# A GRU on one core: the reset gate's two halves in one pass in every step of the middle

## The chip, the cores and the metric

The kernel runs on one core of a Trainium2 chip. The metric is the device time of one execution in microseconds (us), lower is better. Each kernel is timed in several runs, and the median counts. TensorE multiplies matrices into the banks of PSUM, ScalarE applies functions, VectorE does the elementwise work, SyncE starts the transfers. Each engine has its own list of instructions and takes them in the order of that list; semaphores tie the lists together.

## The reference

A gated recurrent unit over 128 steps, batch 64, 512 inputs, 512 hidden values. After every fourth step (but not the last) the state goes through one more layer, the propagation. The output is the states plus the input.

```
def step(h, inp):
    x_t, prop = inp
    comb = jnp.concatenate([x_t, h], axis=-1)
    z = jax.nn.sigmoid(comb @ Wz + bz)
    r = jax.nn.sigmoid(comb @ Wr + br)
    comb2 = jnp.concatenate([x_t, r * h], axis=-1)
    h_cand = jnp.tanh(comb2 @ Wh + bh)
    h_new = (1.0 - z) * h + z * h_cand
    h_next = jnp.where(prop, jnp.tanh(h_new @ Wp + bp), h_new)
    return (h_next, h_new)
...
x = x + transpose(ys)
```

## The kernel before

Everything lies transposed: 512 hidden values are four groups of 128 partitions, the 64 batches are columns. Each float32 matrix is split into a high and a low float16 part, and a product is three: low weights by high values, high weights by high values, high weights by low values.

The steps come in 16 blocks of 8 (BLOCK). In the middle of the kernel the products of x with the input weights, for a whole block, are made by seven products instead of eight (a Strassen scheme), for each of three gates: 21 "stages" of 12 matmuls with 256 columns. They are handed out over the eight steps of the block before (STAGES_AT) and fill TensorE while the recurrence waits for ScalarE and VectorE. A step with t % 4 = 3 does the propagation at its end, and has stages both ahead of it and behind it. ScalarE reads most finished stages out of their banks (`read_stage`, L551), VectorE the products 5 and 6 (`end_quarter`, L963), which add to what ScalarE wrote; a later stage that adds to the same bank waits for that (`wait_stage`: product 7 waits for `c22_out`, which the L963 of product 6 tells). Of the stages, numbers 15 to 17 stand in steps with t % 8 = 6 (17 is a product 5), 18 and 19 ahead of the propagation of a step with t % 8 = 7 (19 is a product 6), and 20 (a product 7) behind it.

One step goes so. TensorE: reset product (R), update product (Z), candidate product (C), stages. `seed` (ScalarE, L613 or L622) puts x's share and the bias into a gate's bank before the product adds to it. The middle of a step is a chain across engines: R is squashed, VectorE multiplies by h and splits the result into high and low (`q_split`, L1048, then L1050 and L1026), and only then can C begin.

A gate can be done in two ways:
- apart: the products by the high and by the low values of h are separate matmuls of 64 columns into one half of a bank, and ScalarE squashes the bank itself (`squash`, L591);
- joint, in steps 19 to 108 (JOINT): `rec_both` (L1362) multiplies the high weights by both parts at once, 128 columns, into both halves of the bank. Then the halves must be added: VectorE does a TENSOR_REDUCE (L1043 in two parts for R, L1061 for Z, L1078 for C), and ScalarE squashes the sum from SBUF (`squash_sums`, L585). The seed fills both halves, with half the value (L613, 512 elements a partition, against L622 with 256).

In these steps Z is always joint, C in t % 8 of 1, 4 and 6, and R where this line says:

```
JOINT_RESET_AT = (0, 1, 2, 4, 5, 6)
```

Where R is joint, TensorE also draws the first 4 matmuls of the step's first stage (AHEAD_OF_C) ahead of C.

The order of work is written out by hand: each engine's list is the loop over steps in its own function, and there is no scheduler. Around the change ScalarE's loop has: squash R, split parts of x (`split_slot`, L539, at the steps in SLOT_AT), squash Z, squash C, `seed(R, t + 1)`, `seed(Z, t + 1)`, then, in a step with a propagation, read the stages ahead of it, squash PROP (tanh), read the stage behind it, and `seed(C, t + 1)`. VectorE's loop has: reduce R if joint, q_split and the rest of q, reduce Z, `split_slot` (L890), reduce C if joint, keep (L1082), new (L1102), the state's high part (L1111, named h_split, or q_split ahead of a propagation), h_ring (L1114), its low part (L1026), then add_states (L1031), a sum of x parts (L950), `end_quarter` (L963), and at a propagation h_split from the tanh (L1141).

Of the kernel before, what the change touches and what calls it, by code (L numbers as in the profile page):

```python
# [16 lines left out]
BLOCK = 8  # L17
RING = 4
R, Z, C, PROP = range(4)
# [13 lines left out]
AHEAD = 32  # L33
REC_SUM_AT = 4
EARLY_PROP_SHARE = 1.4
JOINT_RESET_AT = (0, 1, 2, 4, 5, 6)
AHEAD_OF_C = 4
JOINT = range(19, 109)
JOINT_CANDIDATE_AT = (1, 4, 6)
# [16 lines left out]

STAGES_AT = [((), (0, 1)), ((), (2, 3, 4)), ((), (5, 6)), ((7, 8), (9,)), ((), (10, 11, 12)), ((), (13, 14)), ((), (15, 16, 17)), ((18, 19), (20,))]

SLOT_AT = {2: (5, 6, 6, 8, 8, 9, 10), 3: (4, 5, 6, 7, 7, 8, 9)}
SLOT_AT_LATER = (1, 2, 3, 4, 5, 6, 7)  # L60
SUM_AT = {2: (4, 5, 7, 9), 3: (3, 5, 6, 6)}
SUM_AT_LATER = (0, 1, 5, 3)
# [7 lines left out]
def gru_kernel(nc, x, h0, wz, wr, wh, wp, biases, out):  # L70
# [61 lines left out]
    def fill_of(t):  # L132

        first = issued(t - 1) if t else PER_BLOCK + AHEAD
        return first, (first + issued(t) + 1) // 2, issued(t)

    def stages_of(t):

        m, s = divmod(t, BLOCK)
        return STAGES_AT[s] if m + 1 in SEVEN else ((), ())  # L140
# [9 lines left out]
    def slots_at(t):  # L150

        return [(m, slot) for m in SEVEN for slot, s in enumerate(SLOT_AT.get(m, SLOT_AT_LATER)) if BLOCK * (m - 2) + s == t]

# [17 lines left out]
    def wsum_of(t):  # L171

        return divmod(WSUM_AT.index(t), 4) if t in WSUM_AT else (None, None)
# [6 lines left out]
    with ExitStack() as ctx:  # L180
# [186 lines left out]
        def propagates(t):  # L367
            return t % CHUNK == CHUNK - 1 and t < T - 1

        def joint(t):  # L370

            return t in JOINT

        def joint_reset(t):

            return joint(t) and t % BLOCK in JOINT_RESET_AT

# [4 lines left out]
        def resets_before(t):  # L382
            return sum(joint_reset(step) for step in range(t))
# [10 lines left out]
        def props_before(t):  # L394
            return t // CHUNK
# [103 lines left out]
        def _(act):  # L499
# [42 lines left out]
            def split_wsum(g, n):  # L542

                act.wait_ge(wsum_made, 4 * g + n + 1)
                slot, made = WSUMS[n]
                nc.scalar.activation(win_hi[g][:, slot], made[:], ACT.Copy, scale=scale[:, WIN + g:WIN + g + 1]).then_inc(wsum_hi_ready, 1)
# [34 lines left out]
            def squash_sums(g, func, summed, count, halves):  # L581

                for n, half in enumerate(halves):
                    act.wait_ge(summed, count + n + 1)
                    nc.scalar.activation(gate[g][:, half], gate[g][:, half], func, scale=unscale[:, g:g + 1]).then_inc(gate_ready[g], 1)  # L585

            def squash(g, func, count, halves):

                act.wait_ge(product_done[g], count + 1)
                for half in halves:  # L590
                    nc.scalar.activation(gate[g][:, half, :], acc[g][:, half, :], func, scale=unscale[:, g:g + 1]).then_inc(gate_ready[g], 1)  # L591
# [110 lines left out]
            for t in range(T):  # L702
                m, s = divmod(t, BLOCK)
                first, middle, last = (n // PER_GROUP for n in fill_of(t))
                stages_first, stages_last = stages_of(t)
                wsum_gate, wsum_place = wsum_of(t)


                ahead = t == T - 2
                if joint_reset(t):  # L710
                    squash_sums(R, ACT.Sigmoid, reset_summed, 2 * resets_before(t), HALVES)
                else:
                    squash(R, ACT.Sigmoid, t, HALVES)
                if ahead:
                    seed(R, t + 1)

                if t and t % CHUNK == 0 and props_before(t) < T // CHUNK - 1:
                    seed_prop(props_before(t))
                if wsum_gate is not None:
                    split_wsum(wsum_gate, wsum_place)  # L720
                for block_m, slot in slots_at(t):
                    split_slot(block_m, slot)
                if squares_at(t):
                    act.wait_ge(h_prop_ready, 2 * props_before(t) + 2)
                if t >= BLOCK:
                    for block_m, k in squares_at(t):
                        x_squares(block_m, k)
                if joint(t):
                    squash_sums(Z, ACT.Sigmoid, update_summed, JOINT.index(t), WHOLE)
                else:  # L730
                    squash(Z, ACT.Sigmoid, t, WHOLE)
                if ahead:
                    seed(Z, t + 1)
                if joint_candidate(t):
                    squash_sums(C, ACT.Tanh, candidate_summed, 2 * candidates_before(t), HALVES)
                elif t < T - 1:
                    squash(C, ACT.Tanh, t, HALVES)
                else:
                    for n, half in enumerate(HALVES):
                        act.wait_ge(product_done[C], T + n)  # L740
                        nc.scalar.activation(gate[C][:, half, :], acc[LAST_BANKS[half.start]][:, half, :], ACT.Tanh,  # L741
                                             scale=unscale[:, C:C + 1]).then_inc(gate_ready[C], 1)
                late = [g for g in (R, Z) if starts(t + 1) and groups_for(g, t + 1) > first]
                if t + 1 < T and not ahead:
                    for g in (R, Z):
                        if g not in late:
                            seed(g, t + 1)
                if t < BLOCK:
                    for block_m, k in squares_at(t):
                        x_squares(block_m, k)  # L750
                if s in SPLIT_AT and m + 2 == LAST:
                    for k in SPLIT_AT[s]:
                        split_x(m + 2, k)
                if t in (1, 2):
                    split_rec(PROP, t - 1)
                if t == 2:
                    seed_prop(0)
                if propagates(t):
                    for n in range(first, middle):
                        copy_group(n)  # L760
                        seed_behind(n, late, t + 1)
                    for n in stages_first:
                        read_stage(m + 1, n)
                    act.wait_ge(squares_ready, KC + squares_before(t))
                    squash(PROP, ACT.Tanh, props_before(t), HALVES)
                    for n in range(middle, last):
                        copy_group(n)
                        seed_behind(n, late, t + 1)
                    for n in stages_last:
                        read_stage(m + 1, n)  # L770
                else:
                    for n in range(first, last):
                        copy_group(n)
                        seed_behind(n, late, t + 1)
                    for n in stages_last:
                        read_stage(m + 1, n)
                if t + 1 < T:
                    seed(C, t + 1)
# [725 lines left out]
```

## Time and profile before

| | |
|---|---|
| median of 3 runs | 1040.14 us (1040.03 to 1040.64) |
| the profiled execution | 1041.51 us |
| its span, first to last instruction | 1039.6 us |
| TensorE matmuls | 1034.6 us busy, 20938 |
| VectorE | 872.3 us busy |
| ScalarE | 774.0 us busy |
| a step 3 or 7 of a block in the middle | 9.49 us |

The profile is of one execution. Busy times of TensorE are modelled and overlap: a matmul with 64 columns is shown as 193 ns, though the next starts much sooner. How long one really holds the engine is read from the distance of starts. In the timeline neighbours of one kind are merged to a row with their count. A bracket at a row's end tells of idle time of that engine ahead of it, and of what ended it. The granted clock of TensorE is full (1.0) for the whole span.

### The profile page before, as it was taken

The page shows a single profiled execution, that of the slowest core. Times are in us where ns is not written, and L with a number is a line of the kernel's source. Part 1 is how long each engine was busy: PE and PEld are TensorE (multiplying, and loading weights), DVE is VectorE, ACT ScalarE, POOL GpSimd, SP SyncE. Part 2 cuts the span into 40 slices and gives each one's busy share as a digit, 9 for nine tenths or more (in the row PEclk, how much of TensorE's full clock was granted, in tenths as well). Part 3 has the DMA queues.
Part 4 walks back from the last instruction along what each step waited for, and adds up shares of the span by engine and source line. Part 5 has one row for each costly group of instructions (what it writes and reads, how often), then busy time and mean ns, then how long its engine had stood idle before and what let it go on. Part 6 is the DMA issues. An engine that isn't in the chain of part 4 may idle for free.

```text
span 1039.6 us, 48435 instructions
## 1 busy us (share of the span) xinstructions
PE 1034.6 (100%) x20938; PEld 955.2 (92%) x20938; DVE 872.3 (84%) x2856; ACT 774.0 (74%) x1789; POOL 0.2 (0%) x4
## 2 busy tenths in 40 slices
PE   9999999999999999999999999999999999999998
PEld 4577899999999999999999999999999999999998
DVE  6978888898988899888889888998888998776666
ACT  6877777787877777777877777877777777665565
POOL 0000000000000000000000000000000000000000
PEclk9999999999999999999999999999999999999999
DMA  9312211001111011110011110111100100000001
GB/s 329 112 43 84 84 54 44 21 25 43 43 43 34 12 43 43 44 43 23 23 44 43 43 42 7 41 44 43 44 24 23 43 23 22 24 8 19 24 24 45
DMA packets 38486, 47.29 MB, mean 45 GB/s; under 512 B 2176, under 2 KB 34048, under 8 KB 37888
## 3 DMA queue, kind: packets, MB, share of 16 engines
q1 hardware_dynamic: 38000, 44.12, 12.6%
q8 instruction: 165, 2.70, 1.1%
q14 instruction: 49, 0.40, 0.1%
q10 hardware_dynamic: 272, 0.07, 0.0%
HBM read 27.40 MB, written 16.78 MB: 42 GB/s over the span
## 4 chain that ended last, share of the span: by engine, by line
PE 100%; DVE 0%; issue 0%; ACT 0%; DVEq 0%
PE acc L1354 39%; PE x_acc L1268 34%; PE acc L1362 16%; PE x_acc L1158 8%; PE x_acc L1289 1%; PE acc L1282 0%; PE x_acc L1276 0%; ACT gate L741 0%; DVE new L1093 0%; PE acc L1164 0%; DVE x_blk L1097 0%; DVEq L180 0%; DVE sum_over L967 0%
## 5 line engine op out<-in xcount | busy, mean ns | idle before, releaser
L1268 PE MATMUL x_acc<-x_hi,win_hi 128*128 128x256 f16 x1092 | 297.7, 273 | 0.0
L1268 PE MATMUL x_acc<-x_lo,win_hi 128*128 128x256 f16 x1092 | 297.6, 273 | 0.0
L1268 PE MATMUL x_acc<-x_hi,win_lo 128*128 128x256 f16 x1092 | 297.6, 273 | 0.0
L585 ACT ACTIVATE gate<-gate,unscale 128x128 f32<-128x128 f32 (+1 forms) x292 | 119.8, 435 | 123.7 <-DVE gate L1061 78.2
L591 ACT ACTIVATE gate<-acc,unscale 128x128 f32<-128x128 f32 (+1 forms) x408 | 131.2, 370 | 99.6 <-PE acc L1354 99.4
L1354 PE MATMUL acc<-h_split,wrec_lo 128*128 128x64 f16 x4096 | 181.2, 193 | 0.1
L551 ACT ACTIVATE x_part<-x_acc,bias,part_unscale 128x256 f32<-128x256 f32 x312 | 154.5, 560 | 19.1 <-PE x_acc L1268 19.1
L1362 PE MATMUL acc<-h_split,wrec_hi 128*128 128x128 f16 x2512 | 166.0, 219 | 0.0
L1354 PE MATMUL acc<-q_split,wrec_hi 128*128 128x64 f16 x4000 | 162.0, 193 | 0.3 <-issue 0.3
L1354 PEld LDWEIGHTS acc<-h_split,wrec_lo 128*128 128x128 f16 x4096 | 155.4, 98 | 5.2 <-issue 0.5
L1362 PEld LDWEIGHTS acc<-h_split,wrec_hi 128*128 128x128 f16 x2512 | 142.8, 98 | 0.0
L1354 PEld LDWEIGHTS acc<-q_split,wrec_hi 128*128 128x128 f16 x4000 | 136.5, 98 | 0.4 <-issue 0.4
L1354 PE MATMUL acc<-h_split,wrec_hi 128*128 128x64 f16 x3168 | 134.5, 193 | 0.0
L613 ACT ACTIVATE acc<-x_part,half_seed_scale 128x512 f32<-128x512 f32 x191 | 126.0, 685 | 0.0
L1354 PE MATMUL acc<-q_split,wrec_lo 128*128 128x64 f16 x2544 | 120.6, 193 | 0.0
L1268 PEld LDWEIGHTS x_acc<-x_hi,win_lo 128*128 128x128 f16 x1092 | 106.8, 98 | 11.3
L1268 PEld LDWEIGHTS x_acc<-x_hi,win_hi 128*128 128x128 f16 x1092 | 106.8, 98 | 10.7
L1268 PEld LDWEIGHTS x_acc<-x_lo,win_hi 128*128 128x128 f16 x1092 | 106.9, 98 | 10.1
L1354 PEld LDWEIGHTS acc<-h_split,wrec_hi 128*128 128x128 f16 x3168 | 110.1, 98 | 0.0
L1354 PEld LDWEIGHTS acc<-q_split,wrec_lo 128*128 128x128 f16 x2544 | 98.6, 98 | 5.0
L1048 DVE TENSOR_TENSOR q_split<-gate,h_ring 128x128 f16<-128x128 f32 x192 | 54.3, 292 | 54.2 <-ACT gate L591 46.5
L622 ACT ACTIVATE acc<-x_part,seed_scale 128x256 f32<-128x256 f32 x192 | 88.7, 477 | 1.8
(141 smaller groups left out, 1509.5 us busy)
## 6 DMA issues: line engine op xcount, KB each, us to landing
out_dram<-x_blk SPq DMA_DIRECT2D x30, 512.0 KB, 3.3
x_blk<-x_dram SPq DMA_DIRECT2D x24, 512.0 KB, 3.8
x_blk<-x_dram SPq DMA_DIRECT2D x3, 1024.0 KB, 8.5
x_part<-wz_dram SPq DMA_DIRECT2D x4, 256.0 KB, 6.5
x_part<-wh_dram SPq DMA_DIRECT2D x4, 256.0 KB, 6.3
x_part<-wr_dram SPq DMA_DIRECT2D x1, 1024.0 KB, 10.7
x_part<-wz_dram SPq DMA_DIRECT2D x1, 1024.0 KB, 12.9
x_part<-wh_dram SPq DMA_DIRECT2D x1, 1024.0 KB, 15.4
```

Source lines behind the costliest of these rows:

```text
L551: nc.scalar.activation(part_quarter(m, g, jh, nh)[:, j], in_halves(x_acc[bank][:])[:, j], ACT.Identity, bias=bias[:, g, 2 * jh + j:2 * jh ...
L585: nc.scalar.activation(gate[g][:, half], gate[g][:, half], func, scale=unscale[:, g:g + 1]).then_inc(gate_ready[g], 1)
L591: nc.scalar.activation(gate[g][:, half, :], acc[g][:, half, :], func, scale=unscale[:, g:g + 1]).then_inc(gate_ready[g], 1)
L613: nc.scalar.activation(acc_bank[g][:], added.unsqueeze(1).broadcast_to([P, 2, KC, B]), ACT.Copy, scale=half_seed_scale[:, g:g + 1]).then_i ...
L622: nc.scalar.activation(acc[g], added, ACT.Copy, scale=seed_scale[:, g:g + 1]).then_inc(seed_ready[g], 1)
L1048: nc.vector.tensor_tensor(q_split[:, half, 0, :], gate[R][:, half, :], h_in[:, half, :], ALU.mult).then_inc(q_hi_ready, 1)
L1158: return nc.tensor.matmul(x_acc[bank][:, 0:cols], weights[g][:, 2 * (j // 2) + k // 2, k % 2, j % 2 * P:(j % 2 + 1) * P], values[m % 2][:, ...
L1268: mm = nc.tensor.matmul(in_halves(x_acc[bank][:])[:, j], weights[g][:, slot_w, k, j * P:(j + 1) * P], in_halves(values[m % 2][:, slot_x, : ...
L1289: return nc.tensor.matmul(x_acc[j][:, steps.start * B:steps.stop * B], stage_in(R, k)[:, j * P:(j + 1) * P], x_blk[0][:, k, steps].rearran ...
L1354: mm = nc.tensor.matmul(bank[:, j, :], weights[g][:, k, j * P:(j + 1) * P], values[:, k, lo, :], start=False, stop=False, skip_group_check ...
L1362: mm = nc.tensor.matmul(acc_bank[g][:, :, j, :], wrec_hi[g][:, k, j * P:(j + 1) * P], values[:, k], start=False, stop=False, skip_group_ch ...
```

## The change

Three edits. The reset gate is joint in all steps from 19 to 108, so in the 23 steps with a propagation too. In these same steps the update gate's next seed moves on ScalarE from ahead of the stage reads and the propagation's tanh to behind the tanh. And early in the program (t = 7 and 8, long before the joint steps), one piece of x for block 2 is split in step 7 instead of 8, on ScalarE and VectorE.

```
-JOINT_RESET_AT = (0, 1, 2, 4, 5, 6)
+JOINT_RESET_AT = range(BLOCK)
...
-SLOT_AT = {2: (5, 6, 6, 8, 8, 9, 10), 3: (4, 5, 6, 7, 7, 8, 9)}
+SLOT_AT = {2: (5, 6, 6, 7, 8, 9, 10), 3: (4, 5, 6, 7, 7, 8, 9)}
...
+        def behind_propagation(t):
+
+            return propagates(t) and joint(t) and joint(t + 1)
...
                 if t + 1 < T and not ahead:
                     for g in (R, Z):
-                        if g not in late:
+                        if g not in late and not (g == Z and behind_propagation(t)):
                             seed(g, t + 1)
...
                     squash(PROP, ACT.Tanh, props_before(t), HALVES)
+                    if behind_propagation(t):
+                        seed(Z, t + 1)
                     for n in range(middle, last):
```

The changed file is six lines longer, so its line numbers are 4 (ScalarE's part) or 6 (VectorE's and TensorE's) higher: L963 becomes L969, L1043 becomes L1049, L551 becomes L555.

On VectorE, at the turn from step 30 (t % 8 = 6) to step 31 (t % 8 = 7), before. L963 is the end_quarter of step 30, the row behind it is the first of step 31.

```order
L1026 TENSOR_TENSOR h_split<-h_ring,h_split 128x2x64 [waits h_new_ready,h_hi_ready] x2
L963 SCALAR_TENSOR_TENSOR x_part<-x_acc,part_unscale,x_part 128x2x256 [waits part_unscale_ready,seven_summed,c12_begun]
L1048 TENSOR_TENSOR q_split<-gate,h_ring 128x2x64 [waits gate_ready0] x2
L1050 TENSOR_TENSOR q_full<-gate,h_ring 128x128 x2
L1026 TENSOR_TENSOR q_split<-q_full,q_split 128x2x64 [waits q_full_ready,q_hi_ready] x2
L1061 TENSOR_REDUCE gate<-acc 128x256 [waits product_done1]
```

The same place in the changed kernel:

```order
L1032 TENSOR_TENSOR h_split<-h_ring,h_split 128x2x64 [waits h_new_ready,h_hi_ready] x2
L969 SCALAR_TENSOR_TENSOR x_part<-x_acc,part_unscale,x_part 128x2x256 [waits part_unscale_ready,seven_summed,c12_begun]
L1049 TENSOR_REDUCE gate<-acc 128x128 [waits product_done0]
L1049 TENSOR_REDUCE gate<-acc 128x128
L1054 TENSOR_TENSOR q_split<-gate,h_ring 128x2x64 [waits gate_ready0] x2
L1056 TENSOR_TENSOR q_full<-gate,h_ring 128x128 x2
L1032 TENSOR_TENSOR q_split<-q_full,q_split 128x2x64 [waits q_full_ready,q_hi_ready] x2
L1067 TENSOR_REDUCE gate<-acc 128x256 [waits product_done1]
```

Two reduces of the reset gate have come between the end_quarter of step 30 and q_split.

On ScalarE, the seeds at the end of step 30 and the start of step 31, before (gate_ready0 is the reset gate's, gate_ready1 the update gate's, gate_ready2 the candidate's):

```order
L622 ACTIVATE acc<-x_part,seed_scale 128x256 [waits gate_ready0]
L613 ACTIVATE acc<-x_part,half_seed_scale 128x512 [waits half_seed_scale_ready,gate_ready1]
L551 ACTIVATE x_part<-x_acc,bias,part_unscale 128x256 [waits seven_summed]
L551 ACTIVATE x_part<-x_acc,bias,part_unscale 128x256
L551 ACTIVATE x_part<-x_acc,bias,part_unscale 128x256 [waits seven_summed]
L551 ACTIVATE x_part<-x_acc,bias,part_unscale 128x256
L622 ACTIVATE acc<-x_part,seed_scale 128x256 [waits gate_ready2]
L591 ACTIVATE gate<-acc,unscale 128x128 [waits product_done0]
```

And in the changed kernel:

```order
L617 ACTIVATE acc<-x_part,half_seed_scale 128x512 [waits half_seed_scale_ready,gate_ready0]
L617 ACTIVATE acc<-x_part,half_seed_scale 128x512 [waits half_seed_scale_ready,gate_ready1]
L555 ACTIVATE x_part<-x_acc,bias,part_unscale 128x256 [waits seven_summed]
L555 ACTIVATE x_part<-x_acc,bias,part_unscale 128x256
L555 ACTIVATE x_part<-x_acc,bias,part_unscale 128x256 [waits seven_summed]
L555 ACTIVATE x_part<-x_acc,bias,part_unscale 128x256
L626 ACTIVATE acc<-x_part,seed_scale 128x256 [waits gate_ready2]
L589 ACTIVATE gate<-gate,unscale 128x128 [waits reset_summed] x2
```

The reset gate's seed is now the one with 512 elements, and the squash of the reset gate waits for VectorE's sum (reset_summed), no longer for TensorE's product. Later in step 31, changed kernel, the update gate's seed (the row that waits for gate_ready1) stands behind the two rows of the tanh:

```order
L617 ACTIVATE acc<-x_part,half_seed_scale 128x512 [waits c21_out,half_seed_scale_ready,c11_out,gate_ready0]
L555 ACTIVATE x_part<-x_acc,bias,part_unscale 128x256 [waits seven_summed]
L555 ACTIVATE x_part<-x_acc,bias,part_unscale 128x256
L595 ACTIVATE gate<-acc,unscale 128x128 [waits product_done3,squares_ready]
L595 ACTIVATE gate<-acc,unscale 128x128
L617 ACTIVATE acc<-x_part,half_seed_scale 128x512 [waits c21_out,half_seed_scale_ready,c11_out,gate_ready1]
L555 ACTIVATE x_part<-x_acc,bias,part_unscale 128x256 [waits seven_summed]
```

On TensorE, from the reset product's last part to the candidate's first in step 31, before and then changed:

```order
L1354 MATMUL acc<-h_split,wrec_hi 128x64 [waits h_lo_ready]
L1354 MATMUL acc<-h_split,wrec_hi 128x64 x7
L1354 MATMUL acc<-h_split,wrec_lo 128x64 x8
L1362 MATMUL acc<-h_split,wrec_hi 128x2x64 x16
L1354 MATMUL acc<-q_split,wrec_lo 128x64 [waits q_hi_ready,seed_ready2]
```

```order
L1368 MATMUL acc<-h_split,wrec_hi 128x2x64 [waits h_lo_ready]
L1368 MATMUL acc<-h_split,wrec_hi 128x2x64 x7
L1360 MATMUL acc<-h_split,wrec_lo 128x64 x8
L1368 MATMUL acc<-h_split,wrec_hi 128x2x64 x16
L1274 MATMUL x_acc<-x_hi,win_hi 128x256 [waits first_copied]
L1274 MATMUL x_acc<-x_lo,win_hi 128x256
L1274 MATMUL x_acc<-x_hi,win_lo 128x256
L1274 MATMUL x_acc<-x_hi,win_hi 128x256
L1360 MATMUL acc<-q_split,wrec_lo 128x64 [waits q_hi_ready,seed_ready2]
```

Four matmuls of stage 18 now stand between the update product and the candidate; the stage keeps its other eight behind the candidate.

## Rows read from the trace of the kernel before

**Rows 1.** The page: busy time of the engines, and the chain that ended last.
```profile
PE 1034.6 (100%) x20938; PEld 955.2 (92%) x20938; DVE 872.3 (84%) x2856; ACT 774.0 (74%) x1789; POOL 0.2 (0%) x4
...
PE 100%; DVE 0%; issue 0%; ACT 0%; DVEq 0%
```

**Rows 2.** Timeline, TensorE, step 31: start us, duration us, engine, line, tiles, count.
```profile
291.32 0.40 PE L1354 MATMUL acc<-h_split,wrec_lo 128*128 128x64 f16 x8
...
292.45 0.40 PE L1354 MATMUL acc<-q_split,wrec_lo 128*128 128x64 f16 x8
```

**Rows 3.** Timeline, TensorE, step 26, where the reset gate is joint.
```profile
250.70 0.86 PE L1354 MATMUL acc<-h_split,wrec_lo 128*128 128x64 f16 x24
251.40 1.06 PE L1362 MATMUL acc<-h_split,wrec_hi 128*128 128x128 f16 x16
252.29 0.40 PE L1354 MATMUL acc<-h_split,wrec_lo 128*128 128x64 f16 x8
...
253.42 0.27 PE L1268 MATMUL x_acc<-x_hi,win_hi 128*128 128x256 f16 x1
...
253.86 0.40 PE L1354 MATMUL acc<-q_split,wrec_lo 128*128 128x64 f16 x8
```

**Rows 4.** Timeline, VectorE, the same step 26.
```profile
252.49 0.76 DVE L1043 TENSOR_REDUCE gate<-acc 128x128 f32<-128x256 f32 x2 [0.41 <-PE acc L1362]
253.39 0.62 DVE L1048 TENSOR_TENSOR q_split<-gate,h_ring 128x128 f16<-128x128 f32 x2
...
254.74 0.69 DVE L1061 TENSOR_REDUCE gate<-acc 128x256 f32<-128x512 f32 x1
```

**Rows 5.** Timeline, ScalarE, end of step 30: both seeds and the stage reads.
```profile
288.07 0.46 ACT L622 ACTIVATE acc<-x_part,seed_scale 128x256 f32<-128x256 f32 x1
288.47 0.67 ACT L613 ACTIVATE acc<-x_part,half_seed_scale 128x512 f32<-128x512 f32 x1
289.08 1.91 ACT L551 ACTIVATE x_part<-x_acc,bias,part_unscale 128x256 f32<-128x256 f32 x4
```

**Rows 6.** Timeline, VectorE, step 31, from step 30's L963 to its own.
```profile
291.02 0.75 DVE L963 SCALAR_TENSOR_TENSOR x_part<-x_acc,part_unscale,x_part 128x512 f32<-128x512 f32 x1 [1.22 <-ACT x_part L551]
291.92 0.55 DVE L1048 TENSOR_TENSOR q_split<-gate,h_ring 128x128 f16<-128x128 f32 x2 [0.15 <-ACT gate L591]
...
293.20 0.68 DVE L1061 TENSOR_REDUCE gate<-acc 128x256 f32<-128x512 f32 x1
...
296.93 0.75 DVE L963 SCALAR_TENSOR_TENSOR x_part<-x_acc,part_unscale,x_part 128x512 f32<-128x512 f32 x1
```

**Rows 7.** Timeline, TensorE, step 31: the first matmul of the last stage.
```profile
297.87 0.27 PE L1268 MATMUL x_acc<-x_hi,win_hi 128*128 128x256 f16 x1
```

**Rows 8.** Timeline, step 39: VectorE's L963 and TensorE's last stage.
```profile
360.37 0.74 DVE L963 SCALAR_TENSOR_TENSOR x_part<-x_acc,part_unscale,x_part 128x512 f32<-128x512 f32 x1
...
361.17 0.28 PE L1268 MATMUL x_acc<-x_hi,win_hi 128*128 128x256 f16 x1
```

**Rows 9.** Timeline, VectorE, step 103, the last with t % 8 = 7.
```profile
860.66 0.75 DVE L963 SCALAR_TENSOR_TENSOR x_part<-x_acc,part_unscale,x_part 128x512 f32<-128x512 f32 x1 [1.22 <-ACT x_part L551]
```

**Rows 10.** Timeline, step 27 (t % 8 = 3): VectorE's L963, then ScalarE's tanh and next read.
```profile
258.08 0.74 DVE L963 SCALAR_TENSOR_TENSOR x_part<-x_acc,part_unscale,x_part 128x512 f32<-128x512 f32 x1
...
265.88 0.62 ACT L591 ACTIVATE gate<-acc,unscale 128x128 f32<-128x128 f32 x2 [0.15 <-PE acc L1354]
267.13 1.02 ACT L551 ACTIVATE x_part<-x_acc,bias,part_unscale 128x256 f32<-128x256 f32 x2 [0.63 <-PE x_acc L1268]
```

**Rows 11.** Timeline, steps 8 and 9: two splits, h_split, and TensorE's start into step 9.
```profile
112.13 1.41 DVE L890 SCALAR_TENSOR_TENSOR x_lo<-x_blk,x_scale,x_hi 128x512 f16<-128x512 f32 x2
...
114.32 0.49 DVE L1111 TENSOR_TENSOR h_split<-new,keep 128x128 f16<-128x128 f32 x2
114.39 0.27 PE L1268 MATMUL x_acc<-x_hi,win_lo 128*128 128x256 f16 x1
...
114.75 0.22 PE L1354 MATMUL acc<-h_split,wrec_lo 128*128 128x64 f16 x2
```

## The prediction, made before the changed kernel ran

> **What bounds the kernel now.** I read the page's busy shares and its chain of waits first, then the timeline of TensorE, then those of VectorE and ScalarE in the steps that the change touches. The reader is to see in the first two [rows 1] that TensorE is busy for 100% of the span and that the chain that ended last is TensorE's own work from end to end, while VectorE is at 84%. TensorE waits for nobody to speak of. So taking work off it gains at once, and nothing on VectorE or ScalarE costs anything until it makes TensorE wait. The question for every step is which result TensorE needs, when, and when it comes. I call step 31 and the ten others with t % 8 = 7 from 23 to 103 "sevens" (11 steps), and the twelve with t % 8 = 3 from 19 to 107 "threes". Together they are the 23 steps whose reset gate becomes joint.
>
> **What a joint gate saves on TensorE.** In step 26, already joint, 24 matmuls of 64 columns go from 250.70 to 251.40, 29.2 ns each, and 16 of 128 columns from 251.40 to 252.29, 55.8 ns each [rows 3]. The change replaces 32 of the first by 16 of the second: 934 less 893 ns, 0.04 us a step. For 23 steps that is 0.92 us, as long as TensorE stays fed.
>
> **What feeds the candidate in a joint step.** The gate no longer goes from TensorE's bank straight to ScalarE: VectorE adds the two halves first (two TENSOR_REDUCE), then ScalarE squashes, then VectorE multiplies. Step 26 shows the whole chain [rows 3, 4]: reset product issued until 252.29, first reduce at 252.49 (0.20 later), q_split at 253.39 (0.90 after the reduce), first candidate matmul at 253.86 (1.37 after the reduce). TensorE covers it with the update product, and with four matmuls of the x stage drawn ahead (253.42 to 253.86, 0.44 us). Cover and chain are nearly equal there, so the pattern works only when VectorE is free at the moment the reset product ends.
>
> **Threes.** In step 27 VectorE's last piece of older work (L963) starts at 258.08 and takes 0.74, so it ends at 258.82 [rows 10]; the reset product would be there at about 259.23. VectorE is free, the chain of step 26 holds, no wait: minus 0.04 each. The reduces push VectorE's later work back by about half a microsecond, but TensorE also reaches the propagation only after the drawn-ahead stage work, and the same stretch fits in step 26. On ScalarE the tanh of the propagation starts at 265.88 after a wait for TensorE, and before the next read of a bank (267.13) it is idle for 0.63 [rows 10]. The update gate's seed (0.61 start to start [rows 5]) put behind the tanh fits there: it starts near 266.36, is through at about 267.05, and the next step needs it 16 matmuls after its start at 266.93, at 267.39. Cost nothing, and it takes 0.61 away ahead of the tanh. Without that move the later squash would have pushed the tanh back. Twelve threes: minus 0.48 us.
>
> **Sevens.** Here I find the cost. At the end of the step before (30), ScalarE does seed, seed, four reads of x_acc (L551), and VectorE's L963 of that step waits for the last of them: it starts at 291.02, after 1.22 us idle [rows 5, 6], although step 31 is then nearly through with its reset product (issued until 291.32 [rows 2]). So far that was harmless: the reset gate went past VectorE to ScalarE, and q_split was wanted only at 291.92. Now the two reduces stand behind this L963 in VectorE's order.
> First, the reset seed of step 31 changes from the 256-element form to the 512-element form: 0.40 (288.07 to 288.47) becomes 0.61 (288.47 to 289.08), so the four reads and L963 come 0.21 later [rows 5]: 291.02 + 0.21 = 291.23.
> Second, the next VectorE instruction of this kind starts 0.66 after one of 0.74 to 0.75 (two together 1.41 [rows 11]): first reduce at 291.89. The reset product would be ready at 291.32 - 0.04 + 0.20 = 291.48 [rows 2], so the reduce is 0.41 late.
> Third, TensorE: the candidate is reached at 292.45 - 0.04 + 0.44 = 292.85 [rows 2, 3]. q_split starts at 291.89 + 0.90 = 292.79; its first half takes 0.29, and from VectorE's end to the first matmul of a new block 0.14 pass (step 9: 114.32 + 0.285 to 114.75 [rows 11]), so 293.23. Wait 0.38. The bound from above is step 26's 1.37 [rows 3, 4]: 293.26, wait 0.41.
> Fourth, VectorE is now busy without a break to the end of the step. The update gate's reduce comes 2.25 after the first reset reduce (252.49 to 254.74 [rows 4]), at 294.14 instead of 293.20, and the second L963 comes 3.73 after that (293.20 to 296.93 [rows 6]), at 297.87 instead of 296.93. TensorE's last x stage of the step (L1268 at 297.87 [rows 7]) waits for it. That this wait is real and how long it takes to pass on is seen in step 39, where L963 started at 360.37, ended at 361.11 and the stage's first matmul came at 361.17, 0.06 later [rows 8]. So the stage starts at 297.87 + 0.75 + 0.06 = 298.68 instead of 297.87. TensorE would be there at 297.87 - 0.04 + 0.38 = 298.21 and waits another 0.47. In all a seven is 0.81 longer, the saved 0.04 and the first wait included. The last seven shows the first L963 the same way (860.66, 1.22 idle [rows 9]), and so do the nine between: 11 x 0.81 = 8.9 us. What follows in the step (tanh, h_split, the moved seed) hangs on the propagation, which ends 0.34 later, and the last stage starts 0.81 later, so there is room.
>
> The Trainium skill, page "TensorE: Matmul & The Clock Gate", section on the array and the queue depths, says that ScalarE and VectorE run strictly in order and that only TensorE pulls weight loads ahead. The row agrees as far as it goes: VectorE stood idle for 1.22 us at L963 and started nothing behind it [rows 6], though nothing there was ready yet. If VectorE could take a ready reduce first, sevens would be like threes and rival A's 1039.0 would come out.
>
> **The split of x** goes from step 8 to step 7: one ScalarE copy and one VectorE instruction of 0.66. In step 8 two such stand together (1.41) and step 9 begins late: h_split starts at 114.32, and TensorE's matmuls of 256 columns, 0.11 apart (253.42 to 253.86 is four [rows 3]), break off at 114.39 until 114.75: 0.25 lost [rows 11]. With 0.66 less this goes: minus 0.25 us (between 0 and 0.25). In step 7 VectorE has room until the propagation's input; I take nothing, at most 0.1.
>
> **Sum.** 8.9 - 0.48 - 0.25 = plus 8.2 us. The profiled execution took 1041.51 (span 1039.6), 1.37 above the median of the timed runs, so the same sum gives 1049.7 for a profiled one and 1040.14 + 8.2 = 1048.3 for the median. Its own range: the start of the reduce behind L963 is not shown for this pair (0.60 to 0.75), the seed and the passing on are good to 0.03, so 0.81 may be 0.72 to 0.93: 1047.2 to 1049.6.
>
> **Rivals.** A, not slower: VectorE's hold is hidden after all, and only the saved columns and step 9 count: 0.92 + 0.25 less, 1039.0, within 0.2%. For it: six of eight steps already run this way without a gap [rows 1, 3]. Against it: in step 26 VectorE stood idle for 0.41 ahead of its first reduce [rows 4]; here it is idle too, but because it is held by L963, until 291.02 [rows 6]. It decides at the place of the first L963: with the reduce behind it, it has to start by 291.48 - 0.66 = 290.82, and it starts at 291.23. The Trainium skill, page "Perfetto Trace Analysis", section on the most-contended engine, says to improve the busiest engine first; by that alone the columns saved on TensorE would decide and rival A would hold.
> B, only one wait: the candidate's wait is paid, but the second L963 catches up (VectorE closer packed than before). Then 11 x (0.38 - 0.04) - 0.48 - 0.25 = plus 3.0, 1043.2. Against it: the rows of step 31 from 293.20 to 296.93 tell of no idle time on VectorE that it could give back [rows 6].
> C, more waits: in the threes the chain of step 26 had only some 0.03 to spare (253.39 + 0.29 + 0.14 against 253.86 [rows 3, 4]), and the moved seed has 0.2. If threes wait 0.15 each as well, another 1.8: 1050.1.
> That the change does not do what it says can be left out: the orders show it.
>
> **How the numbers follow.** Forecast 0.80, A 0.09, B 0.06, C 0.05. A measurement of this kernel tells about 0.2% (2.1 us) from no change. Faster would need more than twice what can be saved: 0.02. Same is A without that: 0.08. Slower 0.90. The range takes in the forecast's own, C, and stops short of A and B: 1045.0 to 1050.5.
>
> **What would show it.** In the profile after: in sevens the first reduce of the reset gate directly behind the first L963, 0.4 later than the product allows, and no idle time on VectorE from there to the second L963; TensorE gaps of about 0.4 before the first q_split matmul and 0.5 before the last x stage, 11 times each, and a seven of 10.3 us instead of 9.49. Threes of 9.45 without gaps; step 9 without its gap. If TensorE shows no gaps in sevens, the step that failed is the order on VectorE; if only one gap, the fourth.

## The result, and the profile after

The changed kernel is slower: 1049.73 us median of 5 runs (1048.81 to 1049.94) against 1040.64 for the kernel before beside it (5 runs, 1040.03 to 1042.31), a ratio of 1.0082 with a 95% interval of 1.0072 to 1.0093. The forecast was 1048.3 from 1040.14, a ratio of 1.0078. The profiled executions took 1049.94 and 1041.51, their spans 1048.2 and 1039.6.

The page of the changed kernel, its busy shares and the chain that ended last (answer to [rows 1]):

```profile
PE 1037.1 (99%) x20570; PEld 953.5 (91%) x20570; DVE 889.1 (85%) x2902; ACT 780.6 (74%) x1789; POOL 0.2 (0%) x4
...
PE 77%; DVE 11%; ACT 9%; issue 2%; ACTq 0%; DVEq 0%
```

TensorE has 368 matmuls fewer (23 times 16) and is still said to be busy for 99%. What betrays the change is the chain: it was TensorE's alone, and now a fifth of it runs over VectorE and ScalarE. VectorE's share went up by one point only.

The waits of the whole span name the two places (engine, line, waited for: us in total, times, longest):

```profile
DVE x_part L969 <- ACT x_part L555: 17.3, 13, 1.4
...
PE x_acc L1274 <- DVE x_part L969: 3.3, 11, 0.3
...
PE acc L1360 <- DVE q_split L1054: 2.6, 11, 0.5
```

Both of TensorE's waits stand there 11 times, as often as there are sevens. Their totals are too small by over a third (2.6 and 3.3, where the distances of starts give 11 x 0.37 = 4.1 and 11 x 0.47 = 5.2): the profile models a matmul's end late (0.27 us for one of 256 columns that gives way to the next after 0.11), so idle time after it is shown shortened. True gaps are read from the distance of starts.

The changed kernel's TensorE in step 39, a seven (answer to [rows 2, 7, 8]; start us, duration us; the view ends within the last row, so that row counts only 4 matmuls):

```profile
354.51 0.86 PE L1360 MATMUL acc<-h_split,wrec_lo 128*128 128x64 f16 x24
355.20 1.06 PE L1368 MATMUL acc<-h_split,wrec_hi 128*128 128x128 f16 x16
356.10 0.40 PE L1360 MATMUL acc<-h_split,wrec_lo 128*128 128x64 f16 x8
...
358.04 0.39 PE L1360 MATMUL acc<-q_split,wrec_lo 128*128 128x64 f16 x8 [0.21 <-DVE q_split L1054]
...
363.49 0.28 PE L1274 MATMUL x_acc<-x_hi,win_hi 128*128 128x256 f16 x1 [0.31 <-DVE x_part L969]
...
364.81 0.28 PE L1360 MATMUL acc<-h_split,wrec_lo 128*128 128x64 f16 x4
```

The step lasts 364.81 - 354.51 = 10.30 us instead of 9.49. The reset product is issued until 356.10. From there to the candidate are 24 matmuls of the products (8 of 64 columns, 16 of 128) and 4 of the stage, 1.13 + 0.44 = 1.57, so TensorE was ready at 357.67 and waited 0.37. From 358.04 to the last stage lie 48 + 48 matmuls of 64 columns and 20 of 256, 4.98 us, so it was ready at 363.02 and waited 0.47 more.

VectorE in the same step (answer to [rows 4, 6]):

```profile
356.05 0.75 DVE L969 SCALAR_TENSOR_TENSOR x_part<-x_acc,part_unscale,x_part 128x512 f32<-128x512 f32 x1 [1.44 <-ACT x_part L555]
356.72 0.74 DVE L1049 TENSOR_REDUCE gate<-acc 128x128 f32<-128x256 f32 x2
357.60 0.62 DVE L1054 TENSOR_TENSOR q_split<-gate,h_ring 128x128 f16<-128x128 f32 x2
...
358.94 0.69 DVE L1067 TENSOR_REDUCE gate<-acc 128x256 f32<-128x512 f32 x1
...
362.68 0.75 DVE L969 SCALAR_TENSOR_TENSOR x_part<-x_acc,part_unscale,x_part 128x512 f32<-128x512 f32 x1
363.68 0.54 DVE L1147 TENSOR_SCALAR h_split<-gate,scale 128x128 f16<-128x128 f32 x2 [0.25 <-ACT gate L595]
```

The first L969 is released 1.54 into the step (before: 1.33), the reduce starts 0.67 after it though the product was issued 0.62 before, and from there to the second L969 no row tells of idle time. And ScalarE, whose reads release the first L969 (answer to [rows 5]):

```profile
352.89 1.28 ACT L617 ACTIVATE acc<-x_part,half_seed_scale 128x512 f32<-128x512 f32 x2
354.11 1.91 ACT L555 ACTIVATE x_part<-x_acc,bias,part_unscale 128x256 f32<-128x256 f32 x4
```

Two seeds of the long form take 1.22 from start to the next start, where a short and a long one took 1.01: the 0.21.

A three, step 35: VectorE at the reset gate, ScalarE's tanh and the moved seed (answer to [rows 4, 10]).

```profile
322.93 0.75 DVE L969 SCALAR_TENSOR_TENSOR x_part<-x_acc,part_unscale,x_part 128x512 f32<-128x512 f32 x1
324.09 0.76 DVE L1049 TENSOR_REDUCE gate<-acc 128x128 f32<-128x256 f32 x2 [0.41 <-PE acc L1368]
...
330.70 0.62 ACT L595 ACTIVATE gate<-acc,unscale 128x128 f32<-128x128 f32 x2 [0.19 <-PE acc L1360]
331.21 0.69 ACT L617 ACTIVATE acc<-x_part,half_seed_scale 128x512 f32<-128x512 f32 x1
331.95 1.02 ACT L555 ACTIVATE x_part<-x_acc,bias,part_unscale 128x256 f32<-128x256 f32 x2
```

Here VectorE waits for TensorE before the reduce, not the other way round, and the seed lies between the tanh and the read. The twelve threes take 9.45 each (one 9.449, one 9.451), without a gap.

Where the span's 8.6 us are, by the distances of the steps' first matmuls in both traces: the eleven sevens +8.99 (ten of 10.29 to 10.30, one, step 31, 10.62; before, nine of 9.49 and two of 9.55 and 9.64), the threes -0.48, step 8 -0.29, step 9 -0.08, the steps 30, 56, 57, 77 and 78 together 0.0, ahead of step 0 +0.09, and behind the last matmul +0.32, where a transfer ends the span.

### The profile page after: what moved, and what is told of

It reads as the page before. It is cut to its first block, busy times and chain, and to the rows that moved or that the text cites. A ratio compares the mean times of both kernels' runs of the same rounds, so it can differ in the third digit from the quotient of the medians.

```text
span 1048.2 us, 47768 instructions
## 1 busy us (share of the span) xinstructions
PE 1037.1 (99%) x20570; PEld 953.5 (91%) x20570; DVE 889.1 (85%) x2902; ACT 780.6 (74%) x1789; POOL 0.2 (0%) x4
## 4 chain that ended last, share of the span: by engine, by line
PE 77%; DVE 11%; ACT 9%; issue 2%; ACTq 0%; DVEq 0%
PE acc L1360 30%; PE x_acc L1274 25%; PE acc L1368 13%; PE x_acc L1164 8%; ACT acc L617 3%; ACT x_part L555 3%; ACT gate L589 3%; DVE gate L1067 2%; DVE q_split L1032 2%; DVE x_part L969 1%; PE x_acc L1295 1%; DVE x_lo L896 1%; DVE q_split L1054 1%; DVE gate L1049 1%; DVE q_full L1056 1%
## 5 line engine op out<-in xcount | busy, mean ns | idle before, releaser
L589 ACT ACTIVATE gate<-gate,unscale 128x128 f32<-128x128 f32 (+1 forms) x338 | 136.6, 430 | 145.0 <-DVE gate L1067 77.8
L1368 PE MATMUL acc<-h_split,wrec_hi 128*128 128x128 f16 x2880 | 190.5, 220 | 0.0
L595 ACT ACTIVATE gate<-acc,unscale 128x128 f32<-128x128 f32 (+1 forms) x362 | 117.0, 372 | 89.8 <-PE acc L1360 89.8
L1360 PE MATMUL acc<-h_split,wrec_lo 128*128 128x64 f16 x4096 | 173.9, 194 | 0.0
L1368 PEld LDWEIGHTS acc<-h_split,wrec_hi 128*128 128x128 f16 x2880 | 163.6, 98 | 0.0
L555 ACT ACTIVATE x_part<-x_acc,bias,part_unscale 128x256 f32<-128x256 f32 x312 | 154.6, 561 | 11.3 <-PE x_acc L1274 10.6
L1360 PEld LDWEIGHTS acc<-h_split,wrec_lo 128*128 128x128 f16 x4096 | 152.9, 98 | 4.8
L617 ACT ACTIVATE acc<-x_part,half_seed_scale 128x512 f32<-128x512 f32 x214 | 142.1, 686 | 0.0
L1360 PE MATMUL acc<-h_split,wrec_hi 128*128 128x64 f16 x2432 | 101.9, 194 | 0.0
L1049 DVE TENSOR_REDUCE gate<-acc 128x128 f32<-128x256 f32 x180 | 67.9, 419 | 32.0 <-PE acc L1368 31.9
L1360 PEld LDWEIGHTS acc<-h_split,wrec_hi 128*128 128x128 f16 x2432 | 83.9, 98 | 0.0
```

The lines of the kernel that those rows point to most:

```text
L555: nc.scalar.activation(part_quarter(m, g, jh, nh)[:, j], in_halves(x_acc[bank][:])[:, j], ACT.Identity, bias=bias[:, g, 2 * jh + j:2 * jh ...
L617: nc.scalar.activation(acc_bank[g][:], added.unsqueeze(1).broadcast_to([P, 2, KC, B]), ACT.Copy, scale=half_seed_scale[:, g:g + 1]).then_i ...
L1049: nc.vector.tensor_reduce(flat(gate[R][:, half]), acc_bank[R][:, :, half].rearrange("p n k b -> p (k b) n"), AX_X, ALU.add).then_inc(reset ...
L1360: mm = nc.tensor.matmul(bank[:, j, :], weights[g][:, k, j * P:(j + 1) * P], values[:, k, lo, :], start=False, stop=False, skip_group_check ...
L1368: mm = nc.tensor.matmul(acc_bank[g][:, :, j, :], wrec_hi[g][:, k, j * P:(j + 1) * P], values[:, k], start=False, stop=False, skip_group_ch ...
```

## The experiments

All spans are of the profiled execution, all ratios against the kernel before, timed beside it on the same chip. A step's length is the distance of its first matmul to the next step's.

**e1: the threes alone.**

```
-JOINT_RESET_AT = range(BLOCK)
+JOINT_RESET_AT = (0, 1, 2, 3, 4, 5, 6)
```

> The changed kernel, but the reset gate stays apart in steps with t % 8 = 7; seed and split as changed. My theory (VectorE's end_quarter of step 6 holds the two reduces back in sevens alone): every seven is 9.49 us again, every three 9.45, step 8 and 9 about 0.3 shorter together; against the kernel before minus 0.48 and minus 0.3, so about 0.8 us faster, span near 1038.8. Rival (the two reduces cost VectorE time wherever they stand, the same in all 23 steps): 12 x 0.37 = 4.4 us slower than before.

Measured: sevens 9.49 (median), threes 9.45, step 8 0.29 shorter, span 1038.4, 1.2 us less than before. Two sevens (steps 47 and 95) took 9.71, behind short pauses that the last section takes up, and one three (step 99) took 9.59, for which the trace shows no such pause. Timed 0.9988 (0.9980 to 0.9997), 11 runs. As my theory said; the rival's 4.4 us slower is out. The two reduces cost nothing where VectorE is free when they become due.

**e2: the sevens alone.** The same line with (0, 1, 2, 4, 5, 6, 7).

> The changed kernel, but the reset gate stays apart in steps with t % 8 = 3. My theory: sevens 10.30 us as in the changed kernel, threes 9.49: 8.9 less 0.3 = 8.6 us slower than before, 0.5 more than the changed kernel has over it. Rival (same cost in all 23): 11 x 0.37 = 4.1 us slower.

Measured: sevens 10.30, threes 9.49, span 1048.8, ratio 1.0086 (1.0072 to 1.0100): 8.6 by the theory would be 1.0083. Steps 47 and 95 are 10.64, again behind a pause. The whole loss is in the sevens.

**e5: ScalarE releases VectorE earlier.** Reads of the stages at the end of the step before a seven:

```
-                    for n in stages_last:
+                    for n in (stages_last[1], stages_last[0], *stages_last[2:]) if joint(t) and s == 6 else stages_last:
                         read_stage(m + 1, n)
```

> The changed kernel with the first move alone: ScalarE reads stage 16 before stage 15 at the end of joint steps with t % 8 = 6, so L969 is released 0.9 earlier and the reset reduce starts when the product is there. My theory: no wait at the candidate, but the second L969 still ends late: VectorE's chain from the first reduce is 5.98 long, so the last stage starts 0.40 after its old time: a seven of 9.89, in all 11 x 0.40 - 0.8 = 3.6 us slower than before. Rival (only the first wait is a cause, the second its echo): 9.45 and 0.9 to 1.2 us faster than before.

Measured: sevens 9.89, span 1042.4, ratio 1.0037 (1.0023 to 1.0050). VectorE and TensorE in step 39 of this kernel, which starts at 352.61:

```profile
353.24 0.75 DVE L969 SCALAR_TENSOR_TENSOR x_part<-x_acc,part_unscale,x_part 128x512 f32<-128x512 f32 x1 [0.53 <-ACT x_part L555]
354.40 0.76 DVE L1049 TENSOR_REDUCE gate<-acc 128x128 f32<-128x256 f32 x2 [0.41 <-PE acc L1368]
...
360.38 0.74 DVE L969 SCALAR_TENSOR_TENSOR x_part<-x_acc,part_unscale,x_part 128x512 f32<-128x512 f32 x1
...
361.18 0.28 PE L1274 MATMUL x_acc<-x_hi,win_hi 128*128 128x256 f16 x1 [0.27 <-DVE x_part L969]
```

The first L969 comes 0.91 earlier in the step (0.63 into it, not 1.54) and the reduce waits for TensorE again. The candidate's wait is gone. The second L969 stands 5.98 after the reduce, the length foretold, and still holds the last stage by 0.43. So the wait at the candidate is one thing and that at the last stage another; the second is no echo of the first.

**e6: the second end_quarter ahead of add_states.** In joint steps with a propagation:

```
+                if prop and joint(t):
+                    for n in stages_of(t)[0] + stages_of(t)[1]:
+                        if ORDER[n][1] in (5, 6):
+                            end_quarter(m + 1, n)
                 if prop or t >= T - CHUNK:
                     ...
                     add_states(t, t + 1)
...
-                    if ORDER[n][1] in (5, 6):
+                    if ORDER[n][1] in (5, 6) and not (prop and joint(t)):
```

> The changed kernel with the second move alone: end_quarter ahead of add_states in joint steps with a propagation. My theory: the first wait of 0.38 stays, the second falls from 0.47 to 0.07: a seven of 9.90, in all 3.7 us slower than before. Rival (VectorE has to do the same work by then, the order within it does not matter): 10.30, 8.1 slower.

Measured: sevens 9.90, the first wait 0.37 as in the changed kernel, the second 0.07, span 1043.7, ratio 1.0040 (1.0025 to 1.0055). The order within VectorE's list is worth 0.40 of 0.81, with no work taken away.

**e7: the first end_quarter behind the reset gate.** It is left out at the end of the step before, and put into the seven:

```
+                if s == 7 and joint_reset(t):
+                    for n in stages_of(t - 1)[0] + stages_of(t - 1)[1]:
+                        if ORDER[n][1] in (5, 6):
+                            end_quarter(m + 1, n)
                 wsum_gate, wsum_place = wsum_of(t)
```

> The changed kernel, but the L969 that belongs to step t % 8 = 6 is done in the seven behind the reset gate's reduces and q, not ahead of them. My theory: the first wait goes to 0, but VectorE starts its unbroken stretch 0.25 later than with L969 ahead, so the last stage comes 0.25 later still: one wait of about 1.1 us, a seven of 10.55, in all 10.9 us slower than before. Rival (the wait at the candidate is what costs): 9.45 to 9.9.

Measured: sevens 10.55, span 1050.1, ratio 1.0106 (1.0091 to 1.0121). TensorE in step 39 of this kernel:

```profile
357.08 0.40 PE L1364 MATMUL acc<-q_split,wrec_lo 128*128 128x64 f16 x8
...
361.17 0.39 PE L1364 MATMUL acc<-q_split,wrec_lo 128*128 128x64 f16 x8 [0.34 <-DVE q_split L1121]
...
363.15 0.28 PE L1278 MATMUL x_acc<-x_hi,win_hi 128*128 128x256 f16 x1 [0.42 <-DVE x_part L969]
```

The length is right to 0.01, the shape is not: I foretold one wait of 1.1, there are two, 0.51 at the propagation's input and 0.58 at the last stage. I had followed the last row of VectorE's list and not asked what TensorE wants on the way. What follows stays: the candidate has no wait any more and the kernel is the slowest of all with that seven. The time of VectorE's last piece rules, not the first wait.

**e8: nothing drawn ahead of the candidate in sevens.**

```
+        def draws(t):
+            return joint_reset(t) and t % BLOCK != 7
...
-                    if joint_reset(t):
+                    if draws(t):
                         stage(m + 1, (stages_first + stages_last)[0], stop=AHEAD_OF_C)
```

(`begun` asks `draws` likewise.)

> The changed kernel without the four stage matmuls drawn ahead of the candidate in sevens: TensorE reaches the candidate 0.44 earlier. My theory (the second L969 sets when the seven ends): the first wait grows from 0.38 to 0.81, the second shrinks from 0.47 to 0.03, a seven stays 10.30 and the time the same as the changed kernel's, 8.2 slower than before. Rival (the first wait is the cost): 0.44 more a seven, 10.74, 13 us slower than before.

Measured: sevens 10.29, span 1047.5, ratio 1.0086 (1.0069 to 1.0103). TensorE's candidate and the start of the next step, step 39, which begins at 353.72:

```profile
357.25 0.39 PE L1364 MATMUL acc<-q_split,wrec_lo 128*128 128x64 f16 x8 [0.65 <-DVE q_split L1058]
...
364.01 0.37 PE L1364 MATMUL acc<-h_split,wrec_lo 128*128 128x64 f16 x7
```

The first wait is 0.81 by the starts (0.65 shown), the second 0.03, their sum and the step as before. TensorE may wait early or late; VectorE's chain fixes when the seven ends.

**e9: the seed ahead of the tanh, as before.**

```
-            return propagates(t) and joint(t) and joint(t + 1)
+            return False
```

> The changed kernel, but the update gate's next seed stays ahead of the stage reads and the tanh, as before. Theory: in threes ScalarE now has seed, seed and four reads between the late candidate squash and the tanh, which starts about 0.3 later (near 8.7 us into the step, not 8.4), and TensorE waits some 0.05 to 0.1 for h_split at the start of the next step; in sevens there are only two reads and nothing changes. In all 0.6 to 1.2 us slower than the changed kernel. Rival (the tanh keeps its place because ScalarE was idle enough): no difference in any step.

Measured: the tanh 8.69 into a three instead of 8.40; threes 9.54 instead of 9.45, and the steps behind them 0.07 longer too; sevens 10.30; span 1049.7, 1.5 more than the changed kernel; ratio 1.0097 (1.0082 to 1.0113), whose interval overlaps the changed kernel's. The end of step 27 and the start of step 28:

```profile
266.36 0.65 ACT L595 ACTIVATE gate<-acc,unscale 128x128 f32<-128x128 f32 x2
...
267.02 0.27 PE L1274 MATMUL x_acc<-x_hi,win_lo 128*128 128x256 f16 x1
267.22 0.86 PE L1360 MATMUL acc<-h_split,wrec_lo 128*128 128x64 f16 x24
267.98 0.40 PE L1368 MATMUL acc<-h_split,wrec_hi 128*128 128x128 f16 x4
```

TensorE waits 0.09 for the high part of the state (267.22 instead of 267.13), as expected, and 0.06 again for its low part (24 matmuls take 0.70, the next comes after 0.76), which I had not counted: 12 x 0.165 = 2.0 us instead of 0.6 to 1.2. The moved seed is worth that in the threes.

**e10: the split of x alone.** The kernel before with the second edit of the diff.

> The kernel before with the split in step 7 instead of 8 and nothing else. Theory: the start of step 9 no longer waits for h_split (0.25), the small gap of step 8 goes too; step 7 stays 9485 ns; in all 0.3 us faster in the profile, too little for the timed runs. Rival: step 7 grows by 0.05 to 0.1 because VectorE is 0.33 later at the propagation's input.

Measured: step 7 9.485 as before, step 8 6.85 instead of 7.13 (-0.29), step 9 8.13 instead of 8.68. That -0.55 is no gain of the edit: the step had 0.56 of gaps inside it before, and they come and go in kernels that are alike up to there (0.48 in the changed kernel, none in e4 and e8, 0.13 to 0.52 in the others of e1 to e9). Timed 0.9999 (0.9990 to 1.0007): too little to time. The 0.29 is the start of step 9 (0.25) and a small gap in step 8.

**e3: both moves, e5 and e6 together.**

> The changed kernel with two moves: at the end of a joint step with t % 8 = 6 ScalarE reads stage 16 before stage 15, so that VectorE's end_quarter (L969) is released two reads (0.9 us) earlier; and in joint steps with a propagation VectorE does the end_quarter ahead of add_states (0.4 earlier). My theory: both waits go but for 0.03; a seven takes 9.48, a three 9.45, in all 0.8 us faster than before. Rival (the first wait is cost by the two reduces themselves, not by the held L969): the sevens keep a wait of 0.3 to 0.4 and the kernel stays 3 to 4 us slower than before.

Measured: sevens 9.50, threes 9.45, one wait of 0.04 at the last stage, span 1038.2, timed 0.9992 (0.9983 to 1.0001), 11 runs. Of a seven's 0.85 of waits 0.05 are left, and it is within 0.01 of its old 9.49, with the reset gate joint everywhere. The last L969 of step 31 in this kernel, which begins at 288.45, and the stage behind it:

```profile
290.24 0.76 DVE L1049 TENSOR_REDUCE gate<-acc 128x128 f32<-128x256 f32 x2
...
293.09 0.74 DVE L896 SCALAR_TENSOR_TENSOR x_lo<-sum_b,x_scale,x_hi 128x512 f16<-128x512 f32 x1
...
295.82 0.75 DVE L969 SCALAR_TENSOR_TENSOR x_part<-x_acc,part_unscale,x_part 128x512 f32<-128x512 f32 x1
...
296.63 0.28 PE L1278 MATMUL x_acc<-x_hi,win_hi 128*128 128x256 f16 x1
```

**e4: and the split of x behind add_states in sevens.**

```
-                for block_m, slot in slots_at(t):
+                for block_m, slot in slots_at(t) if not (joint(t) and t % BLOCK == 7) else ():
                     split_slot(block_m, slot)
...
                     add_states(t, t + 1)
+                for block_m, slot in slots_at(t) if joint(t) and t % BLOCK == 7 else ():
+                    split_slot(block_m, slot)
```

> As e3, and in sevens VectorE's split of x (0.66) also goes behind add_states. My theory: VectorE is now 0.66 ahead of the last stage's need, no wait at all in sevens: 9.45 each, 23 x 0.04 + 0.3 = 1.2 us faster than before, 0.1%, within what a measurement tells; the profile shows it. Rival: something else in the seven ends late (the tanh, the seed behind it) and it stays above 9.49.

Measured: sevens 9.52 (step 47, 9.80, is the exception), longer than in e3, span 1039.6, timed 1.0001 (0.9992 to 1.0010). VectorE in step 31 of this kernel, which begins at 288.58:

```profile
292.61 0.69 DVE L1067 TENSOR_REDUCE gate<-acc 128x256 f32<-128x512 f32 x1
293.87 0.42 DVE L1088 SCALAR_TENSOR_TENSOR keep<-gate,h_ring 128x256 f32<-128x256 f32 x1 [0.58 <-ACT gate L589]
...
297.01 0.74 DVE L896 SCALAR_TENSOR_TENSOR x_lo<-sum_b,x_scale,x_hi 128x512 f16<-128x512 f32 x1
297.67 0.47 DVE L1153 TENSOR_SCALAR h_split<-gate,scale 128x128 f16<-128x128 f32 x2
```

And ScalarE's copy, the only thing that this split (L896) waits for:

```profile
291.47 0.71 ACT L543 ACTIVATE x_hi<-sum_b,x_scale 128x512 f16<-128x512 f32 x1
```

My expectation failed. Where the split had stood, VectorE now idles for 0.58 until ScalarE has squashed the update gate: the split had filled a wait and cost nothing there. Behind add_states it runs until the tanh is due, and h_split comes directly behind it, about 0.02 too late for the next step. The last stage keeps its wait of 0.04.

## Why the prediction was right

Step by step, in its own order:

- **The saved columns**: 0.04 a step foretold, 9.450 against 9.490 in each of the twelve threes. Right.
- **Threes**: no waits foretold, none found. The seed behind the tanh costs nothing; without it the kernel would lose another 2.0 us by the lengths of the steps (e9; the timed runs do not tell the two apart). Rival C is out for the changed kernel.
- **Sevens, first and second term**: L963 later by 0.21 (found 1.54 against 1.33 into the step), the reduce 0.66 after it (found 0.67; the pair was not to be seen before, and I had allowed 0.60 to 0.75).
- **Third**: a wait of 0.38 at the candidate; found 0.37.
- **Fourth**: the second L963 holds the last stage by 0.47 more; found 0.47. A seven of 10.30: found 10.29 to 10.30 in ten of eleven. Step 31 is the one that I missed, by 0.32: a pause of VectorE in step 30 that no row of before showed there (last section).
- **The split of x**: 0.25 foretold, 0.29 found in step 8, another 0.08 in step 9 that is not its own.
- **Sum**: +8.2 foretold. On its own terms the traces give 11 x 0.81 = 8.9 for the sevens, -0.48 for the threes and -0.29 for step 8: 8.1. The other 0.4 it did not have: 0.3 more in step 31, 0.2 less because steps 39 and 87 were long before, -0.08 in step 9, +0.09 ahead of step 0 and +0.32 behind the last matmul. The span grew by 8.6; the ratio of the timed runs says 8.5 (1.0082 of 1040.6), with 7.5 to 9.7 inside its interval. So the mechanism is borne out by the lengths of the steps. That the total agrees to 0.3 is partly luck: the stretch ahead of step 0 alone lay between 0.59 shorter and 0.36 longer than before in the traces of e1 to e10.

Rival A fell with the 22 gaps, and with e1 against e2. It was right on one thing: the pattern with all eight steps joint can run (e3), if VectorE's older work is out of the way. Rival B (the candidate's wait alone) fell by e5, which has no such wait and still loses 0.40 a seven, and by e8, where that wait doubles and the time stays. No term of the sum fell. Two readings were loose and moved no number: 2.1 us is 1.8 times the 1.17 that can be saved, not more than twice, and the chances of the forecast, B and C add up to 0.91, not to the 0.90 given for slower. One argument does not hold, that of the ready reduce, below. The 0.21 by which the longer seed delays L963 is read from both traces; no run changed the seed alone.

The two rules weighed there. The prediction says that sevens would be like threes if VectorE could take a ready reduce first. They do not test that. In step 39 of the changed kernel L969 starts at 356.05, and the reset product, issued until 356.10, was due at 356.30 by step 26's 0.20. VectorE was at work when the reduce became ready, and the reduce came directly behind, at 356.72. The prediction's own times say the same (L963 at 291.23, the product at 291.48): an engine free to choose would have taken L963 first too. What bears on the rule is e4. There VectorE stands idle for 0.58 at L1088 until 293.87, though the split (L896) further down its list was ready: ScalarE's copy had ended at 292.18, and in e3 the split ran at 293.09. VectorE did not take it until 297.01. That agrees with what the Trainium skill says of VectorE's queue, in "TensorE: Matmul & The Clock Gate", on the queue depths.

The other rule, in the Trainium skill's "Perfetto Trace Analysis", on the most-contended engine, would have sent the reader to TensorE first, by its matmuls (100%) as by its weight loads (92%), against VectorE's 84%. TensorE's work did shrink, by 0.04 a step in 23 steps, and the kernel lost 0.81 in each of eleven steps through the less busy engine.

## What to carry to other kernels

When an engine's part of a chain is enlarged, look first at what stands just ahead of it in that engine's own list, and at what releases that; the busy share over the span, 84% before and 85% after, told nothing of it here. Follow the enlarged list to its end, since the last thing that it hands over may be missed by more than the first, and then ask at each hand-over on the way, not at the last alone. Before moving work away from a busy engine's list, check whether it lies in a wait: the split of x did, and moving it made things worse.

## What the runs showed of the hardware that was not expected

TensorE's start after the end of the releasing VectorE instruction is not one figure. At the last stage it took 0.06 us (L969 ends at 363.43, matmul at 363.49), at the candidate 0.15 (q_split's first half, 0.29 long, from 357.60, matmul at 358.04), and 0.15 again at the propagation's input in e7. What makes the difference, no run here shows. Where a chain has only 0.03 to spare, as in the threes, it decides.

VectorE sometimes pauses for about 0.3 us and waits for nothing that the profile shows ("issue"). In the changed kernel that falls into step 30, between the two halves of q's low part:

```profile
285.77 0.28 DVE L1032 TENSOR_TENSOR q_split<-q_full,q_split 128x128 f16<-128x128 f32 x1
286.31 0.29 DVE L1032 TENSOR_TENSOR q_split<-q_full,q_split 128x128 f16<-128x128 f32 x1 [0.26 <-issue]
```

The second half starts 0.54 after the first instead of 0.20, and step 31 grows by 0.32. It is at the same place in e3 to e9, whose lists on VectorE are alike up to there. Step 31 is 10.62 in e8 and e9 and 10.22 in e6, 0.32 over the other sevens there; in e3, e4 and e5, whose sevens have slack ahead of the reset gate, and in e7 it costs nothing. In e1 and e2, whose lists are another, steps 47 and 95 are the long ones, in e7 step 103. Before, the long steps 39 and 87 cost 0.06 and 0.15, because there VectorE had time in hand.

Counting the records of VectorE's list in the traces, those of its sequencer included, gives these pauses an address. From step 19 on, the twelve traces have 75 pauses of 0.09 to 0.26 us put down to "issue", and the instruction behind each has a number that leaves 64 or 65 when divided by 128 (960 for the one above; 1472 and 2880 in e1 and e2; 3137 in step 103 of e7). Most such places show no pause. So a pause keeps its place while the list ahead of it is the same, and another one comes up when instructions are added; what it is, no run here shows. Slack taken from an engine is paid for in such pauses too.
